# A fused transformer kernel on one core: GpSimd's weight splits in four parts, row normalising moved to ScalarE, the last attention turns reordered

## The chip, the cores and the metric

The kernel runs on one core of one Trainium2 chip. The metric is the device time of one execution in microseconds, as the median of several executions. The core has five engines that run their own instruction streams and wait for one another by semaphores: TensorE (PE in the rows, its weight loads PEld), VectorE (DVE), ScalarE (ACT), GpSimd (POOL) and SyncE (SP), which here issues the DMAs.

## The reference

`x` is 16 sequences of 128 tokens with 256 features. Four residual blocks follow one another:

```python
x = x + tanh(g_xattn[0]) * attention16(layernorm(x), ctx)     # 16 heads, biases, output projection
x = x + tanh(g_ffn[0])   * moe8_dense(layernorm(x))           # 8 experts, all tokens through all experts
x = x + tanh(g_xattn[1]) * attention1(layernorm(x), ctx, mask)# one head of 256
x = x + tanh(g_ffn[1])   * switch(layernorm(x))               # top-1 of 8, capacity 256 rows an expert
```

In the dense mixture each token has eight routing weights. They come from a sigmoid of the router's logits: an exponential of the distance to 1/e inside a zone, a normalised best two where no expert is in the zone, and then a division by their sum. Each expert is `(silu(x Wg) * (x Wu)) Wd` with 256 hidden features. In the last block a token goes to the expert with the largest logit, if it is among the first 256 tokens of that expert, through `relu(x w1) w2` with 1024 hidden features; its result is multiplied by the gate's softmax value.

## The kernel before, in words

Every float32 product is made of three products of "fp32r" halves: a high half (rounded copy) and a low half (difference), so each tensor that TensorE reads is split first. `product` (line 1591) runs the three. Splitting is a copy for the high half and a subtraction for the low one. ScalarE makes the high half of what leaves PSUM (`..._high`, `..._evict`), VectorE the low half (`..._low`); GpSimd makes both halves of the dense experts' weights in `gate_up_split` (1024 columns, lines 2145 and 2147) and `down_split` (512 columns, lines 2153 and 2155), which SyncE then keeps in HBM and reloads for later token groups. The order of work is written out by hand, per engine. Every engine runs its instructions strictly in that order.

The stages:

- **First attention**, steps `b` = 0 to 15, one sequence each, from the start to about 450 us. For each half of the heads TensorE computes scores twice, VectorE takes their maxima (`maximum`, line 1010), GpSimd turns those into a diagonal matrix (`diagonals`, line 2135), which a matmul subtracts, and ScalarE takes the exponential (line 593). `norm1` on VectorE then normalises the row for the experts with a root found by Newton steps (lines 1047 and 1048, three times). `x1_low` (line 1056) hands it to TensorE. From b = 4 the **dense experts** run in between: `gate_up`, `silu`, `h_mult`, `h_high`, `h_low`, `down`, `accumulate` (line 1079), for four groups of four sequences. `zones`, `two_best` and `expert_weights` (lines 1124 to 1145) make a group's routing weights on VectorE, many short instructions in a chain; the first `accumulate` of a group waits for them. `small_ready` (line 937) splits the router weights at b = 4 on VectorE.
- **Experts 25 to 31** of the last group, about 450 to 562 us, with the second attention of groups 0 and 1 begun in between.
- **`turn3`**, three turns `(ga, gb)` = (2, 1), (3, 2), (None, 3), about 562 to 638 us. For `gb`: `probs_transpose`, `attend` (line 1962), `add_attention`, `moments_b`, `root_b` (lines 262 to 267), `normalise_b` (line 1366), `xb_transpose`, `logits1`, `pick_expert` (its last result is `oh_b`), `count_experts`, `places`, `pick_place` (its result is `tok_idx`, line 1418). For `ga`: the projections `k1`, `q1`, `v1`, `scores1`, `mask_and_max`, exponentials. `dispatch` on GpSimd then scatters each token's row (with its scale and shift) to its expert's slot in HBM by indirect DMAs (line 2224).
- **Switch experts**, from about 646 us: SyncE loads the slots back (line 535, first four tiles, then twelve), VectorE normalises two tiles (`slots_norm`, line 1531), TensorE transposes them and runs `hidden` (48 matmuls) and `down4` (48 matmuls, line 2097) per expert, and GpSimd scatters the results (line 2245). ScalarE splits the expert's weights (`split`, line 746), GpSimd (`split_w1`, line 2214) and VectorE (`split_w2`, line 1541) make the low halves, 2048 columns each.

## Time and profile before

| | |
|---|---|
| median of 3 executions | 764.35 us (763.16 to 766.68) |
| the profiled execution | 764.7 us, span 762.9 us from first to last instruction |
| mean granted TensorE clock | 0.921 of full |
| busy: TensorE | 646.4 us (85%) |
| busy: VectorE | 521.0 us (68%) |
| busy: ScalarE | 331.2 us (43%) |
| busy: GpSimd | 229.1 us (30%) |

Busy times are sums of instruction durations without overlap. A share over the whole span mixes stages with different limits, so the stages are read one by one in the timeline. In timeline rows the number in square brackets is the engine's idle time before the instruction, and behind the arrow is what ended it. A clock of 1.00 is 2.4 GHz, 0.50 is 1.2 GHz.

### The profile page before, as it was taken

The page shows a single profiled execution, that of the slowest core. Times are in us where ns is not written, and L with a number is a line of the kernel's source. Part 1 is how long each engine was busy: PE and PEld are TensorE (multiplying, and loading weights), DVE is VectorE, ACT ScalarE, POOL GpSimd, SP SyncE. Part 2 cuts the span into 40 slices and gives each one's busy share as a digit, 9 for nine tenths or more (in the row PEclk, how much of TensorE's full clock was granted, in tenths as well). Part 3 has the DMA queues.
Part 4 walks back from the last instruction along what each step waited for, and adds up shares of the span by engine and source line. Part 5 has one row for each costly group of instructions (what it writes and reads, how often), then busy time and mean ns, then how long its engine had stood idle before and what let it go on. Part 6 is the DMA issues. An engine that isn't in the chain of part 4 may idle for free.

```text
span 762.9 us, 12648 instructions
## 1 busy us (share of the span) xinstructions
PE 646.4 (85%) x4564; PEld 546.7 (72%) x4564; DVE 521.0 (68%) x1362; ACT 331.2 (43%) x530; POOL 229.1 (30%) x155
## 2 busy tenths in 40 slices
PE   5978598899899899999799889999966931799995
PEld 4656366787678778778688777898855821799995
DVE  6877987677877866866776647479458883466662
ACT  4434155355356456456355325152523321455641
POOL 2444624566532212221014010010031242255542
PEclk9879779899999999999999999999989955799998
DMA  7303303335442242333243424434221141964700
GB/s 225 121 15 127 125 1 139 125 135 211 180 166 83 85 165 84 137 113 125 83 165 113 162 87 152 132 124 146 83 69 43 61 161 43 318 210 153 242 20 26
DMA packets 43463, 94.51 MB, mean 124 GB/s; under 512 B 3519, under 2 KB 24383, under 8 KB 42384
## 3 DMA queue, kind: packets, MB, share of 16 engines
q1 hardware_dynamic: 41344, 87.62, 33.6%
q0 software_dynamic: 2064, 6.16, 2.3%
q8 instruction: 33, 0.54, 0.3%
q14 instruction: 22, 0.18, 0.1%
HBM read 72.94 MB, written 21.04 MB: 123 GB/s over the span
## 4 chain that ended last, share of the span: by engine, by line
PE 65%; DVE 24%; issue 5%; ACT 2%; DMA 1%; POOL 1%; DVEq 0%; SPq 0%; ACTq 0%; POOLq 0%
PE psum L1591 43%; PE psum L2097 6%; PE psum L1668 2%; PE psum L1698 2%; PE psum L1628 2%; PE psum L1662 2%; DVE work L1063 1%; DVE scratch L266 1%; DVE x_all L1079 1%; PE psum L1635 1%; PE psum L1647 1%; DVE work L951 1%; PE psum L1962 1%; PE psum L1893 1%; PE psum L1945 1%
## 5 line engine op out<-in xcount | busy, mean ns | idle before, releaser
L1591 PE MATMUL psum<-arena 128*128 128x256 f32 (+1 forms) x2544 | 446.0, 334 | 33.8 <-DVE x_all L1079 15.6
L1591 PEld LDWEIGHTS psum<-arena 128*128 128x128 f32 x2544 | 384.5, 199 | 78.4 <-DVE x_all L1079 14.8
L2135 POOL TENSOR_TENSOR diag<-neg_ident,work 128x1024 fp32r<-128x1024 f32 x32 | 60.9, 1904 | 249.3 <-DVE work L1010 242.5
L1063 DVE TENSOR_TENSOR work<-work,psum 128x512 f32<-128x512 f32 x64 | 43.9, 686 | 62.1 <-PE psum L1591 57.3
L625 ACT ACTIVATE arena<-work 128x512 fp32r<-128x512 f32 x64 | 40.3, 630 | 90.7 <-DVE work L1063 78.7
L1079 DVE SCALAR_TENSOR_TENSOR x_all<-psum,w_exp,x_all 128x256 f32<-128x256 f32 x128 | 55.9, 479 | 27.7 <-PE psum L1591 26.9
L618 ACT ACTIVATE work<-psum 128x512 f32<-128x512 f32 x64 | 38.2, 597 | 56.8 <-PE psum L1591 56.3
L1068 DVE TENSOR_TENSOR arena<-work,arena 128x512 fp32r<-128x512 f32 x64 | 51.8, 810 | 8.7 <-ACT arena L625 8.2
L2218 POOL TENSOR_TENSOR arena<-work,arena 128x1024 fp32r<-128x1024 f32 x4 | 9.5, 2370 | 151.1 <-ACT arena L641 151.1
L1010 DVE TENSOR_REDUCE work<-psum 128x8 f32<-128x1024 f32 x32 | 39.0, 1220 | 15.7 <-PE psum L1647 15.6
L593 ACT ACTIVATE work<-psum 128x1024 f32<-128x1024 f32 x32 | 32.8, 1026 | 35.4 <-PE psum L1668 32.3
L2097 PE MATMUL psum<-arena 128*128 128x256 f32 x384 | 47.9, 284 | 0.0
L2097 PEld LDWEIGHTS psum<-arena 128*128 128x128 f32 x384 | 46.6, 192 | 0.0
L2214 POOL TENSOR_TENSOR arena<-work,arena 128x2048 fp32r<-128x2048 f32 x8 | 37.0, 4621 | 15.9 <-ACT arena L746 15.9
L880 ACT ACTIVATE arena<-psum 128x256 fp32r<-128x256 f32 x64 | 22.6, 385 | 44.1 <-PE psum L1591 43.5
L1545 DVE SCALAR_TENSOR_TENSOR arena<-psum,arena 128x256 fp32r<-128x256 f32 x64 | 24.9, 421 | 20.2 <-ACT arena L880 19.0
L618 ACT ACT_TABLE_LOAD x26 | 33.4, 1283 | 0.5
L746 ACT ACTIVATE arena<-work 128x2048 fp32r<-128x2048 f32 x16 | 30.5, 1907 | 5.1 <-DMA work<-in_w 5.1
L1662 PE MATMUL psum<-arena 32*128 32x256 f32 x384 | 32.6, 303 | 0.2 <-DVE arena L1003 0.2
L2245 POOL DMA_INDIRECT out<-work,out_idx x16 | 15.8, 990 | 51.0 <-DVE work L1556 48.5
L2224 POOL DMA_INDIRECT slots<-x_all,tok_idx x16 | 16.8, 1048 | 42.4 <-DVE tok_idx L1418 38.7
L1662 PEld LDWEIGHTS psum<-arena 32*128 32x128 f32 x384 | 25.9, 192 | 0.8 <-issue 0.8
(194 smaller groups left out, 844.8 us busy)
## 6 DMA issues: line engine op xcount, KB each, us to landing
arena<-kept SPq DMA_DIRECT2D x24, 1024.0 KB, 5.6
work<-in_w SPq DMA_DIRECT2D x16, 1024.0 KB
kept<-arena SPq DMA_DIRECT2D x8, 1536.0 KB, 6.1
arena<-kept SPq DMA_DIRECT2D x24, 512.0 KB, 4.8
work<-in_w SPq DMA_DIRECT2D x8, 768.0 KB, 7.8
slots<-fill POOLq DMA_DIRECT2D x1, 2080.0 KB
work<-in_ctxT SPq DMA_DIRECT2D x8, 256.0 KB, 3.0
work<-in_ctxT SPq DMA_DIRECT2D x4, 512.0 KB, 5.2
```

What stands on the lines that cost most here:

```text
L593: act.activation(probs[u % 2], ps[:, ST:ST + 2, :].rearrange("p j (h q) -> p (j h) q", q=P), ACT.Exp, scale=DH ** -0.5).then_inc(ex, 1)
L618: act.activation(gu[i % 2], ps[:, GA, :], ACT.Silu).then_inc(sl, 1)
L625: act.activation(hT[n % 2][0][:, m, :], gu[i % 2], ACT.Copy).then_inc(hh, 1)
L1010: dve.tensor_reduce(mx[u % 2], ps[:, MX:MX + 2, :].rearrange("p j (h k) -> p (j h) k", k=P), AX.X, ALU.max).then_inc(mx_ok, 1)
L1063: dve.tensor_tensor(gu[i % 2], gu[i % 2], ps[:, UP, :], ALU.mult).then_inc(hm, 1)
L1068: dve.tensor_tensor(hT[n % 2][1][:, m, :], gu[i % 2], hT[n % 2][0][:, m, :], ALU.subtract).then_inc(hl, 1)
L1079: ins = dve.scalar_tensor_tensor(x_all[:, g * GB + t, 0:D], ps[:, DN, j * D:(j + 1) * D], w_exp[g % 2][:, t, e:e + 1], x_all[:, g * GB + t ...
L1591: mm = pe.matmul(dst, left(i, k), right(j, k), start=(n == 0), stop=(n == 3 * K2 - 1))
L1662: pe.matmul(ps[:, ST + j, m * 256:(m + 1) * 256], kT[h % 2][i][r:r + 32, m, t:t + P], qM[h % 2][jj][r:r + 32, m, :, t:t + P], start=False, ...
L2097: mm = pe.matmul(ps[:, 4 + i, j * D:(j + 1) * D], h4[i][a][:, f, j * P:(j + 1) * P], w4[i][b][:, 1, f * D:(f + 1) * D], start=(f == 0 and ...
L2135: pool.tensor_tensor(diag, neg_ident[:, :].rearrange("p (o q) -> p o q", o=1).to_broadcast([P, 8, P]), mx[u % 2].rearrange("p (h o) -> p h ...
L2214: pool.tensor_tensor(w4[i][1][:, 0, :], raw4[i][:, 0, :], w4[i][0][:, 0, :], ALU.subtract).then_inc(w4_l1.sem, 1)
```

## The change

1. **GpSimd's splits in parts.** `gate_up_split` and `down_split` call `split_parts`: four copies and then four subtractions, each over a quarter of the columns. Waits on the counts are multiplied by `PARTS` = 4.
2. **Router weights.** Their zeroing, copy and subtraction go from VectorE's `small_ready` (b = 4) to GpSimd's `router_ready` (b = 1).
3. **Root of `norm1`.** The second instruction of each Newton step becomes a `tensor_scalar` whose last operand is a per-row scalar, in place of a `scalar_tensor_tensor` with a second tensor.
4. **Routing weights.** The first division by the sum and both clampings fall away, and the last division, the gate and the write are one instruction.
5. **Normalising on ScalarE.** `normalise_a`, `normalise_b` and `slots_norm` (but for the first two tiles) become ScalarE activations with a scale and a shift; VectorE makes the shift with one short instruction. The bias of `v1` is added to `x_all` by GpSimd (`value_bias`; rows of the softmax sum to one), so that `v1` is only copied, by ScalarE (`v1_evict`). Row numbers come from constants, so `row_numbers` and three short instructions per turn fall away.
6. **Order of `turn3`.** On TensorE `xa_transpose` and `k1_project` of the next group go to the end of the turn before; `q1_project` comes ahead of `v1_project`, and `scores1` ahead of `xb_transpose`. VectorE does `stats_a`, `moments_a`, `root_a` first in the turn and `mask_and_max` before `xb_low`.
7. **`keep_warm`.** 11 matmuls of 512 bf16 columns, whose results are not used, in the second turn, 35 in the third, and 44 behind it.
8. **First split of the switch experts.** Both low halves for expert 0 are made by VectorE (`first_split`), the second after all rows are dispatched; ScalarE makes both high halves in the last turn.
9. **Slots.** They are loaded in three DMAs (tiles 0 and 1, 2 and 3, the rest).
10. **End.** The last `down4` writes its two halves to different banks and signals the first by itself; `scatter` waits for each half by itself.

The core of the diff:

```diff
+            def split_parts(n, a, z, high, low):
+                i, step = n % 2, (z - a) // PARTS
+                for c in range(a, z, step):
+                    pool.tensor_copy(w2s[i][0][:, c:c + step], raw[i][:, c:c + step]).then_inc(high, 1)
+                for m, c in enumerate(range(a, z, step)):
+                    pool.wait_ge(high, PARTS * n + m + 1)
+                    pool.tensor_tensor(w2s[i][1][:, c:c + step], raw[i][:, c:c + step], w2s[i][0][:, c:c + step], ALU.subtract
+                                       ).then_inc(low, 1)
...
+            def router_ready():
+                pool.wait_ge(s_small, 16 * 7)
+                for i in range(2):
+                    pool.memset(wr[i].bitcast(F32), 0.0).then_inc(s_wr0, 1)
+                pool.wait_ge(s_wr0, 2)
+                pool.tensor_copy(wr[0][:, :, :, 0:E], wr_raw).then_inc(s_wr0, 1)
+                pool.wait_ge(s_wr0, 3)
+                pool.tensor_tensor(wr[1][:, :, :, 0:E], wr_raw, wr[0][:, :, :, 0:E], ALU.subtract).then_inc(s_wr, 1)
...
+            def value_bias(g):
+                pool.wait_ge(s_bo, 2)
+                for t in range(g * GB, (g + 1) * GB):
+                    pool.wait_ge(na, t + 1)
+                    pool.tensor_tensor(x_all[:, t, 0:D], x_all[:, t, 0:D], bv1r, ALU.add).then_inc(xv, 1)
+
             ctx_low(0)
+            value_bias(0)
+            value_bias(1)
+            ctx_low(1)
+            value_bias(2)
             pool.wait_ge(s_disp, 16)
...
+            ctx_low(2)
+            dispatch(0)
+            value_bias(3)
+            ctx_low(3)
+            dispatch(1)
+            dispatch(2)
+            dispatch(3)
...
                 for _ in range(3):
                     step(dve.tensor_scalar(u, r, t, r, ALU.mult, ALU.mult))
-                    step(dve.scalar_tensor_tensor(r, u, 1.5, r, ALU.add, ALU.mult))
+                    step(dve.tensor_scalar(r, u, 1.5, r, ALU.add, ALU.mult))
...
             def expert_weights(g):
-                divide_by_sum(7)
                 seq(dve.tensor_tensor(r[7], r[7], over_e(rs[1]), ALU.mult))
                 seq(dve.tensor_tensor(rt[4], rt[4], rt[7], ALU.add))
-                divide_by_sum(4)
+                seq(dve.tensor_reduce(rs[2], r[4], AX.X, ALU.add))
+                seq(dve.reciprocal(rs[2], rs[2]))
                 if g >= 2:
                     dve.wait_ge(ac, 2 * E * (g - 1))
-                dve.tensor_scalar(w_exp[g % 2], r[4], tgate[:, 2:3], None, ALU.mult).then_inc(s_wexp, 1)
+                dve.scalar_tensor_tensor(w_exp[g % 2], r[4], tgate[:, 2:3], over_e(rs[2]), ALU.mult, ALU.mult
+                                         ).then_inc(s_wexp, 1)
...
+            def normalise_a(g):
+                act.wait_ge(sa, g + 1)
...
+                for t in range(g * GB, (g + 1) * GB):
+                    act.activation(xn_a[t % GB], x_all[:, t, 0:D], ACT.Identity, bias=shiftA[:, t:t + 1], scale=rstdA[:, t:t + 1]
+                                   ).then_inc(na, 1)
...
             def turn3(ga, gb):
+                more = ga is not None and ga + 1 < G
                 probs_copy(gb)
                 if ga is None:
                     act.wait_ge(a1, 2 * G)
                     split(0, 0, 0)
+                    split(0, 0, 1)
                 else:
-                    xa_high(ga)
-                    k1_evict(ga)
                     q1_evict(ga)
+                    if more:
+                        normalise_a(ga + 1)
+                    v1_evict(ga)
+                normalise_b(gb)
                 xb_high(gb)
...
+            def keep_warm(n):
+                for _ in range(n):
+                    pe.matmul(ps[:, 0, :], ident_b[:, :], hide[:, 0:1, :].to_broadcast([P, 4, P]), start=True, stop=True,
+                              skip_group_check=True)
+
             def turn3(ga, gb):
+                more, last = ga is not None and ga + 1 < G, ga is None
                 probs_transpose(gb)
-                if ga is not None:
-                    xa_transpose(ga)
+                if last:
+                    keep_warm(2)
                 attend(gb)
-                if ga is not None:
-                    k1_project(ga)
+                if last:
+                    keep_warm(22)
+                else:
+                    q1_project(ga)
                     v1_project(ga)
-                    q1_project(ga)
+                    scores1(ga)
                 xb_transpose(gb)
-                if ga is not None:
-                    scores1(ga)
+                if more:
+                    xa_transpose(ga + 1)
+                else:
+                    keep_warm(5)
                 logits1(gb)
+                if not more:
+                    keep_warm(2)
                 logits1_transpose(gb)
+                if more:
+                    k1_project(ga + 1)
+                else:
+                    keep_warm(4)
                 places(gb)
+            xa_transpose(2)
+            k1_project(2)
             turn3(2, 1)
             turn3(3, 2)
             turn3(None, 3)
+            keep_warm(44)
...
+                        if more and f == 3:
+                            act.wait_ge(s_xs[1 + i], 16)
+                            slots_norm(*nxt)
```

## Rows read from the trace of the kernel before

**Rows 1.** Stages: us; busy of PE, PEld, DVE, ACT, POOL; clock; DMA.

```profile
72.00:100.00 28.00, 18.85 (x138) 12.76 (x136) 24.97 (x64) 6.77 (x12) 15.87 (x14) 0.75 0.33 114
100.00:136.00 36.00, 29.13 (x195) 22.86 (x193) 28.79 (x79) 18.42 (x30) 12.15 (x9) 0.93 0.20 74
136.00:450.00 314.00, 292.98 (x2176) 242.34 (x2176) 223.92 (x561) 157.45 (x226) 92.39 (x65) 0.98 0.38 134
450.00:563.00 113.00, 103.60 (x598) 90.39 (x597) 71.30 (x200) 43.71 (x72) 11.09 (x7) 0.97 0.34 114
608.00:648.00 40.00, 12.23 (x49) 8.23 (x48) 23.37 (x74) 8.71 (x17) 13.38 (x9) 0.55 0.29 96
```

**Rows 2.** Timeline, 82 to 92 us: start us, us, engine, line, operation, idle before.

```profile
82.14 0.28 DVE L1047 TENSOR_SCALAR work<-work 128x1 f32<-128x1 f32 x1
82.17 2.36 POOL L2147 TENSOR_TENSOR arena<-work,arena 128x1024 fp32r<-128x1024 f32 x1
82.45 2.10 DVE L1048 SCALAR_TENSOR_TENSOR work<-work 128x1 f32<-128x1 f32 x1
...
85.15 1.03 ACT L593 ACTIVATE work<-psum 128x1024 f32<-128x1024 f32 x1 [2.20 <-PE psum L1668]
...
91.41 1.65 PE L1591 MATMUL psum<-arena 128*128 128x256 f32 x6 [2.20 <-DVE arena L1025]
```

**Rows 3.** GpSimd's groups: count, busy us, mean ns, idle before.

```profile
L2147 POOL TENSOR_TENSOR arena<-work,arena 128x1024 fp32r<-128x1024 f32 x8 | 19.4, 2423 | 0.6
...
L2160 POOL TENSOR_TENSOR x_all<-x_all,biasr 128x256 f32<-128x256 f32 x16 | 12.2, 764 | 0.0
```

**Rows 4.** Timeline, the first group's routing, 117 to 140 us.

```profile
122.50 2.22 DVE L1097 TENSOR_TENSOR work<-work 128x32 f32<-128x32 f32 x1
...
136.24 9.34 PE L1591 MATMUL psum<-arena 128*128 128x256 f32 x48 [2.88 <-DVE x_all L1079]
```

**Rows 5.** Timeline, the second group's routing, 254 to 262 us.

```profile
254.80 0.18 DVE L1103 TENSOR_REDUCE work<-work 128x4 f32<-128x32 f32 x1
...
258.26 4.00 PE L1591 MATMUL psum<-arena 128*128 128x256 f32 x31 [2.59 <-DVE x_all L1079]
```

**Rows 6.** Timeline, four scaled copies on ScalarE and two bf16 matmuls.

```profile
29.46 1.70 ACT L586 ACTIVATE arena<-arena,parity 128x256 fp32r<-128x256 f32 x4
...
35.39 0.61 PE L1628 MATMUL psum<-hide,ident_b 128*128 128x512 bf16 x2
```

**Rows 7.** Timeline of the second and third turns, 591 to 639 us.

```profile
591.50 0.21 PE L1986 MATMUL psum<-oh_b,tri_b 128*128 128x32 bf16 x1 [6.27 <-DVE oh_b L1398]
...
594.25 2.18 PE L1962 MATMUL psum<-work 128*128 128x256 f32 x8
...
613.44 3.78 PE L1962 MATMUL psum<-work 128*128 128x256 f32 x8 [0.69 <-ACT work L780]
...
618.51 1.91 ACT L746 ACTIVATE arena<-work 128x2048 fp32r<-128x2048 f32 x1 [5.13 <-DMA work<-in_w]
...
620.51 4.49 POOL L2214 TENSOR_TENSOR arena<-work,arena 128x2048 fp32r<-128x2048 f32 x1 [1.51 <-ACT arena L746]
620.63 4.38 DVE L266 SCALAR_TENSOR_TENSOR scratch<-scratch,work 128x4 f32<-128x4 f32 x1
...
630.33 2.90 PE L1591 MATMUL psum<-arena 128*128 128x512 f32 x6 [1.46 <-ACT arena L787]
...
638.06 0.16 DVE L1418 TENSOR_TENSOR tok_idx<-work,tokn 128x4 int32<-128x4 f32 x1
```

**Rows 8.** GpSimd's dispatches (ns min/median/max), slots' first load, first expert.

```profile
L2224 POOL DMA_INDIRECT slots<-x_all,tok_idx x16: 964/969/2112, 555.8 to 643.5; - x16
...
646.11 3.75 DMA x_all<-slots
...
653.60 8.67 PE L1591 MATMUL psum<-arena 128*128 128x256 f32 x48 [1.80 <-DVE arena L1536]
```

**Rows 9.** Timeline, the last scatter.

```profile
757.17 0.98 POOL L2245 DMA_INDIRECT out<-work,out_idx  x1 [0.30 <-issue]
```

More of the change, by code:

```diff
@@ L335, in block_kernel @@
         oh1, loc1, dest = sem("onehot_ready"), sem("places_ready"), sem("rows_ready")
-        s_xs = [sem("first_slots_loaded"), sem("other_slots_loaded")]
+        s_xs = [sem(f"{n}_slots_loaded") for n in ("first", "second", "other")]
         s_raw4 = [sem(f"expert1_weights_loaded{i}") for i in range(2)]
@@ L827, in _ @@
             silu(29, 1)
+            v1_evict(1)
             h_high(29, 1)
+            normalise_b(0)
+            xb_high(0)
             silu(30, 0)
-            xb_high(0)
             h_high(30, 0)
@@ L862, in turn3 @@
                 gate_exp(gb)
+                if more:
+                    xa_high(ga + 1)
+                if more:
+                    k1_evict(ga + 1)
+            xa_high(2)
+            k1_evict(2)
             turn3(2, 1)
@@ L880, in hidden, with slots_norm @@
                 act.activation(h4[i][0][:, f, :], ps[:, f % 4, 0:CAP], ACT.Relu).then_inc(h1_hi.sem, 1)
+            def slots_norm(g, i):
+                for j in range(2):
+                    row = xs[:, bass.ds(4 * g + 2 * i + j, 1), :].rearrange("p a c -> p (a c)") if not isinstance(g, int) \
+                        else xs[:, 4 * g + 2 * i + j, :]
+                    act.wait_ge(xd_t.sem, xd_t.now(g, 1) if i else xd_t.before(g, 2))
+                    act.activation(xd[j], row[:, 0:D], ACT.Identity, bias=row[:, D + 1:D + 2], scale=row[:, D:D + 1]
+                                   ).then_inc(xd_ok.sem, 1)
             def turn(g, last):
@@ L1380, in xb_low @@
                                       ).then_inc(nb_lo, 1)
-            top, rank, gate, row, place, own = (r3s[i] for i in range(6))
+            top, rank, gate, row, place = (r3s[i] for i in range(5))
             def over8(col):
@@ L1513, in turn3 @@
                     root_a(ga + 1, 1)
-                    normalise_a(ga + 1)
+                attention_gates(gb)
+                add_attention(gb)
+                moments_b(gb)
+                root_b(gb)
+                if ga is not None:
+                    mask_and_max(ga)
+                xb_low(gb)
+                if ga is None:
+                    first_split(0, w4_l1.sem)
                 pick_expert(gb)
-                count_experts(gb)
+                slot_and_gate(gb)
                 pick_place(gb)
+                if more:
+                    xa_low(ga + 1)
+            xa_low(2)
             turn3(2, 1)
@@ L2091, in down4 @@
                 pe.wait_ge(y4.sem, y4.before(g, i + 1))
+                if last:
+                    pe.wait_ge(y4.sem, y4.now(g, 1))
                 for j in range(2):
+                    bank = 4 if last and j else 4 + i
                     for f in range(8):
@@ L2106, in turn @@
                         slots_transposed(*((g, 1) if i == 0 else (g + 1, 0)))
-                    down4(g, i)
+                    down4(g, i, last and i == 1)
             slots_transposed(0, 0)
```

221 lines of the change are left out of this document (94 added, 127 removed).

## Prediction

> **What bounds it.** I read the busy time and the granted clock by stage first [rows 1], and then the timeline wherever TensorE stands idle. From 136 to 450 us TensorE is busy 293 of 314 us: only its rare waits can be won there. Before that, and from 563 to 653 us, VectorE sets the end. From 608 to 648 TensorE works 12 of 40 us at 0.55 of its clock, which is the lower level (1.2 GHz) for nearly all of it. So each edit is asked one thing: does it shorten a wait of TensorE in one of these stretches? The last stage, from 653 us, is TensorE's again.
>
> **72 to 100 us.** In [rows 2] the second `L1048` (VectorE, one element, two tensor inputs from SBUF) takes 2.10 us, and it ends with GpSimd's `L2147`. `L1047` beside it, the same size with scalars in place of the second tensor, takes 0.28. So the scalar form of the root update saves some 2 us of VectorE here. It has a price: against the 0.16 us of an undisturbed `L1048` I take +0.07, between 0 and the 0.12 by which `L1047` is longer. That is 0.2 us per norm, and some five of the sixteen norms are on the path: +1.0 (0 to +1.8). The router weights leave VectorE too: `small_ready` stands before `o_low(3)`, and TensorE starts at 91.41 having waited 2.20 us for it [rows 2]. Of both savings not all arrives. ScalarE's exponential (85.15, 1.03 us [rows 2]) stands before `x1_high` and so holds `x1_low`; through `o_normalise` and `o_back`, `out_project` then starts near 89.1 instead of 91.4: **-2.3** (-3.5 to 0). On GpSimd `router_ready` is about 1.6 us (four small instructions, by [rows 3]) at b = 1, where GpSimd waits for VectorE's maxima: nothing.
>
> **The four parts.** A subtraction of 1024 columns takes 2.42 us, one of 256 takes 0.76 [rows 3], so some 0.2 us is fixed per instruction. Twelve more instructions per expert are up to 2.5 us, 20 us of GpSimd for eight experts, less what overlaps. GpSimd works 12 of 36 us and 92 of 314 [rows 1], so this is covered unless VectorE is held by it. What VectorE wins is less than it looks. Before, one small two-input operation lost 2 us and the next ones were free (`L1097` at 122.50, 2.22 us [rows 4]); now each meets a part of its own and loses some 0.5. Only a large one, 0.7 us by itself and held for 2, wins clearly. TensorE waited 2.88 us behind this chain [rows 4]; I take -0.7 there (0 to -3.9), and -1.0 (0 to -3) for the rest up to 250 us. The Trainium skill (SBUF — State Buffer, Who interferes with whom) says that the side which issues first keeps the shared port pair for its whole instruction while the other blocks fully, and that a VectorE instruction with at most one SBUF input, outside the 2-port modes, does not contend. The rows of `L1048` and `L1047` agree; by that rule alone a chain of small operations gains nothing, and this term would be 0 instead of -0.7.
>
> **Expert weights.** `expert_weights` falls from eleven VectorE instructions to five, each about 0.22 us with the gap behind it (`L1103` takes 0.18 [rows 5]): -1.35 us. TensorE waits 2.59 us for the accumulation behind it [rows 5], and nothing else stands close behind. Four groups: **-5.4**. With fewer waits before 140 us the clock, at 0.75 over 72 to 100 [rows 1], may stay up longer; -1.0 (0 to -4).
>
> **450 to 563 us.** ScalarE takes `normalise_a` (four at 1.70 us by [rows 6]) and `v1_evict`; GpSimd takes `value_bias`, 16 x 0.76 = 12.2 us [rows 3]. TensorE sets this stage (it waits for few things), so the moves gain nothing. They cost something at its end: behind `silu(31,1)`, `normalise_a(2)` delays `h_high(31,1)` and so `down(31,0)` by 0.7 us, and `value_bias(2)` and `ctx_low(2)` may hold VectorE: +1.0 (0 to +2).
> To 563 us: -2.3 +1.0 -0.7 -1.0 -5.4 -1.0 +1.0 = **-8.4**.
>
> **The three turns of turn3.** Marks of before: `attend(2)` ends at 596.4, `attend(3)` at 617.2, the last `tok_idx` is begun at 638.06 [rows 7].
> - First turn, -2.8. `xa_transpose(2)` and `k1_project(2)` go where TensorE waited for the exponentials. VectorE does `stats_a(3)` and its root ahead of group 1's chain, and `value_bias(3)` can hold that chain: `logits1(1)` is 1.1 us later. But TensorE's wait of 6.27 us for `oh_b` [rows 7] was caused by the same work standing before `pick_expert`; `k1_project(3)` (3.0 us) now fills half of it. That is -6.3 +3.0 +1.1 = -2.2; the transposes of `xa` (1.9) are gone from before `attend(2)`, but `probs_copy(2)` waits for `k1_evict(3)` (+1.3).
> - Second turn, -2.6. `k1_project` (-3.0) and `xa_transpose` (-1.9) are gone from it; 5 warming matmuls (two take 0.61, overlapped, so 0.22 each [rows 6]) and the later ones add 1.1; `v1_evict` before `normalise_b` on ScalarE waits for `v1_project`: +1.2.
> - Third turn, -6.7, from 21.0 us. GpSimd's first subtraction of 2048 columns (4.49 us) held `L266` for 4.38 [rows 7]: -4.2. It is now on VectorE behind `xb_low` and fits into logits, copy and transposes (3.1 us). `logits1(3)` took 2.90 at the lower clock [rows 7], 1.5 at the full one: -1.4. The other transposes and matmuls at full clock give -0.7, three VectorE instructions fewer -0.6, ScalarE's slower normalising +0.2. Its two splits (1.91 each) need weights that landed some 10 us after their issue (ScalarE waited 5.13 us for them, to 618.51 [rows 7]); issued near 601 they are there before the normalising.
> Together **-12.1** (-15 to -4).
>
> **Dispatch and first slots.** One dispatch took 2.11 us where the median is 0.97 [rows 8], while VectorE ran `L1541`; that subtraction now waits until the dispatch is over: **-1.1**. Two tiles of slots instead of four land some 0.9 us sooner (3.75 us for four), the transposes at full clock take 0.5 less, and the first 48 matmuls 5.8 instead of 8.67 [rows 8]. Against this, ScalarE's split behind the second `hidden` comes some 1.6 us before expert 1's weights, whose load starts no sooner after the dispatch: it is late next, and costs 2.0. Sum **-2.3** (-4.5 to 0). From there each half turn is TensorE's; `slots_norm` on ScalarE (0.9 us behind the fourth `hidden`) is done before the transposes need it: 0.
>
> **Tail.** The last two row scatters were issued 0.98 + 0.30 = 1.28 us apart [rows 9], after both tiles; now the first goes during the second half of `down4`, and one of two sums (0.45) is off the end too: **-1.7**.
>
> **Sum.** -8.4 -12.1 -1.1 -2.3 -1.7 = -25.6 on the profiled execution's 764.7 us (span 762.9 and 1.8 around it): 739.1. The median shown is 0.35 lower; I say **739**.
>
> **Rivals.**
> (a) Chance 0.17, about 731: the stalls and the lower clock before 140 us go almost wholly (another -6), and the weights are in time (-2). For it: TensorE's waits there are larger than what I take.
> (b) Chance 0.15, about 748: the order written for ScalarE becomes the wait. `v1_evict` stands before `normalise_b` and waits for TensorE; if each turn loses 3 us to such queues, 9 of the 12 us are lost. Against it: ScalarE worked only 9 of the 40 us from 608 [rows 1].
> (c) Chance 0.08, about 751: the clock stays low in spite of the warming matmuls. Then 22 of them take 10 us and 44 take 20, past the arrival of the slots by 8, and the clock's gains (4) are lost: +12.
> (d) Chance 0.05, the other side, about 771: the 20 us (parts) and 12.2 us (bias) that GpSimd adds fall on VectorE, each two-input operation waiting for one of its instructions. Whole, it gives 739 + 32. It decides only if over four fifths of that time is on the path; against it, most of it runs where TensorE is the bound.
>
> Mine has 0.55, in 733 to 745. Case (a) reaches to 727, (b) and (c) to 752; outside remain (d) and the edges. What a measurement of this kernel can tell from no change is about 0.5%, 3.8 us: only (d) gives the same or slower, split 0.02 and 0.03.
>
> **What would show it.** No `L1048` over 0.3 us; GpSimd's parts at 0.4 to 0.8 us with short VectorE stalls; 1.3 us of wait before a group's first accumulation; the last `tok_idx` near 618 (638.1 - 8.4 - 12.1); the full clock from the last `attend` to the first slots; one scatter after the last matmul. It would be wrong if the last turn waits in ScalarE's queue, if warming matmuls still run when the slots are there, or if TensorE has new waits for VectorE between 136 and 450.

## The result, and the profile after

The changed kernel takes 737.8 us (737.4 to 743.0, four executions) against 763.8 (761.9 to 766.7): ratio 0.967, interval 0.962 to 0.971. The forecast was 739, in a range of 727 to 752. A second set of six gave 740.6 (732.9 to 742.3) against 760.6, ratio 0.970 (0.965 to 0.974).

The profiled execution of the changed kernel is its slowest (743.0, span 741.2), so its span fell by 21.7 us where the medians fell by 26.0 (and by 20.0 in the second set). Why executions of one program differ is part of the findings. The stages of the changed kernel, columns as in [rows 1]:

```profile
72.00:100.00 28.00, 19.76 (x151) 13.56 (x150) 24.93 (x66) 8.73 (x13) 19.30 (x26) 0.85 0.42 147
100.00:136.00 36.00, 30.18 (x202) 24.16 (x201) 29.41 (x76) 17.96 (x29) 15.86 (x28) 0.93 0.21 74
136.00:450.00 314.00, 296.41 (x2186) 245.09 (x2185) 216.40 (x547) 160.87 (x232) 105.82 (x134) 0.97 0.38 135
450.00:563.00 113.00, 105.23 (x617) 91.03 (x616) 66.48 (x189) 54.60 (x99) 16.72 (x17) 1.00 0.36 119
...
604.00:632.00 28.00, 21.99 (x101) 10.29 (x99) 14.02 (x42) 7.32 (x11) 5.75 (x6) 0.92 0.30 94
632.00:643.00 11.00, 9.51 (x56) 9.30 (x57) 2.91 (x8) 5.53 (x12) 3.08 (x1) 0.73 1.06 368
```

GpSimd works 105.8 us between 136 and 450 (92.4 before, [rows 1]), and TensorE is none the worse for it: it is busy for 296.4 us against 293.0. The last two rows are the new weak places: the clock is 0.92 in the last turn and 0.73 in the first slots' matmuls.

The groups of the root and of GpSimd's parts (columns as in [rows 3]), in which the root's second instruction is now `L1101` and the subtraction `L2190`:

```profile
L1100 DVE TENSOR_SCALAR work<-work 128x1 f32<-128x1 f32 x48 | 13.1, 273 | 1.7
...
L1101 DVE TENSOR_SCALAR work<-work 128x1 f32<-128x1 f32 x48 | 10.3, 214 | 1.7
...
L2190 POOL TENSOR_TENSOR arena<-work,arena 128x256 fp32r<-128x256 f32 x32 | 25.3, 819 | 0.0
...
L2190 POOL TENSOR_TENSOR arena<-work,arena 128x128 fp32r<-128x128 f32 x32 | 13.7, 459 | 0.0
```

No instruction of `norm1`'s root is held any more, where [rows 2] had one of 2.10 us. The price is 0.214 - 0.16 = 0.05 us each; I had taken 0.07. A quarter of the subtraction takes 0.82 us, not 2.42 / 4 = 0.61.

TensorE's waits before each group's first accumulation, in the timeline:

```profile
133.95 8.22 PE L1609 MATMUL psum<-arena 128*128 128x256 f32 x41 [1.94 <-DVE x_all L1132]
...
252.60 7.34 PE L1609 MATMUL psum<-arena 128*128 128x256 f32 x48 [1.59 <-DVE x_all L1132]
...
368.95 1.68 PE L1609 MATMUL psum<-arena 128*128 128x256 f32 x12 [1.48 <-DVE x_all L1132]
...
472.59 9.66 PE L1609 MATMUL psum<-arena 128*128 128x256 f32 x64 [1.20 <-DVE x_all L1132]
```

The first two answer to [rows 4, 5], which have 2.88 and 2.59; in all four groups before the waits were 2.88, 2.59, 2.83 and 2.83, and they are now 4.9 us shorter in sum. The turns, in the timeline, with `L1980` the matmuls of `attend` and `L2067` the warming ones:

```profile
591.22 2.06 ACT L776 ACTIVATE work<-x_all 128x256 f32<-128x256 f32 x4
...
592.32 1.47 PE L1911 MATMUL psum<-cst,work 128*128 128x128 f32 x8
...
601.00 1.99 PE L1980 MATMUL psum<-work 128*128 128x256 f32 x8 [0.26 <-ACT work L812]
...
602.84 4.91 PE L2067 MATMUL psum<-hide,ident_b 128*128 128x512 bf16 x22
...
609.09 2.11 PE L1911 MATMUL psum<-cst,work 128*128 128x128 f32 x8 [1.35 <-ACT work L776]
...
612.78 2.35 PE L1609 MATMUL psum<-arena 128*128 128x512 f32 x6
...
619.34 0.16 DVE L1440 TENSOR_TENSOR tok_idx<-work,cst 128x4 int32<-128x4 f32 x1
```

The last `tok_idx` is at 619.3 where [rows 7] have 638.1. The first transposes of `xb` in the second turn (592.32) follow scores without a gap, although ScalarE's normalising ahead of them was behind `v1_evict`. And the first slots: timeline first, with the warming matmuls (617.77), the transposes, the first `hidden` matmuls and ScalarE's split (`L762`), then one piece of the chain that ended last:

```profile
617.77 9.66 PE L2067 MATMUL psum<-hide,ident_b 128*128 128x512 bf16 x44
...
629.44 0.66 PE L2112 MATMUL psum<-cst,work 128*128 128x128 f32 x4 [2.01 <-DVE work L1549]
...
631.90 7.22 PE L1609 MATMUL psum<-arena 128*128 128x256 f32 x36 [1.81 <-DVE arena L1554]
...
637.92 1.91 ACT L762 ACTIVATE arena<-work 128x2048 fp32r<-128x2048 f32 x1 [2.67 <-DMA work<-in_w]
...
640.61 1.71 PE L1609 MATMUL psum<-arena 128*128 128x256 f32 x12 [1.49 <-DVE arena L1563]
```

```profile
627.48 10.33 DMA work<-in_w
```

What released the split is a weight load that takes 10.3 us of the chain. [rows 8] had the slots' load there instead. The end, in the timeline, against [rows 9]:

```profile
732.61 0.98 POOL L2313 DMA_INDIRECT out<-work,out_idx  x1 [6.35 <-DVE work L1579]
...
735.42 0.98 POOL L2313 DMA_INDIRECT out<-work,out_idx  x1 [1.82 <-DVE work L1579]
```

One scatter is left behind the last matmul (734.0).

### The profile page after: what moved, and what is told of

Same layout as the page of the kernel before. It is cut to its first block, busy times and chain, and to the rows that moved or that the text cites. A ratio compares the mean times of both kernels' runs of the same rounds, so it can differ in the third digit from the quotient of the medians.

```text
span 741.2 us, 12936 instructions
## 1 busy us (share of the span) xinstructions
PE 659.5 (89%) x4654; PEld 548.0 (74%) x4654; DVE 485.6 (66%) x1269; ACT 356.4 (48%) x584; POOL 252.2 (34%) x270
## 4 chain that ended last, share of the span: by engine, by line
PE 62%; DVE 23%; issue 6%; ACT 4%; DMA 2%; POOL 1%; ACTq 0%; SPq 0%; DVEq 0%; POOLq 0%
PE psum L1609 41%; PE psum L2139 6%; PE psum L1716 2%; PE psum L1686 2%; PE psum L1646 2%; PE psum L1680 2%; DVE x_all L1132 2%; DVE work L1116 2%; PE psum L1653 1%; DMA work<-in_w 1%; DVE work L1004 1%; PE psum L1665 1%; DVE work L1100 1%; PE psum L1723 1%; DVE scratch L266 1%
## 5 line engine op out<-in xcount | busy, mean ns | idle before, releaser
L1116 DVE TENSOR_TENSOR work<-work,psum 128x512 f32<-128x512 f32 x64 | 43.8, 685 | 66.1 <-PE psum L1609 60.3
L1121 DVE TENSOR_TENSOR arena<-work,arena 128x512 fp32r<-128x512 f32 x64 | 48.8, 763 | 10.1 <-ACT arena L630 9.7
L2290 POOL TENSOR_TENSOR x_all<-x_all,biasr 128x256 f32<-128x256 f32 x16 | 11.2, 732 | 85.5 <-ACT work L648 85.5
L2190 POOL TENSOR_TENSOR arena<-work,arena 128x256 fp32r<-128x256 f32 (+1 forms) x64 | 38.9, 639 | 0.0
L2273 POOL TENSOR_TENSOR arena<-work,arena 128x2048 fp32r<-128x2048 f32 x7 | 32.5, 4646 | 15.4 <-ACT arena L762 15.4
L762 ACT ACTIVATE arena<-work 128x2048 fp32r<-128x2048 f32 x16 | 30.4, 1905 | 4.8 <-DMA work<-in_w 2.7
```

Of the source, the lines that this page charges most:

```text
L1116: dve.tensor_tensor(gu[i % 2], gu[i % 2], ps[:, UP, :], ALU.mult).then_inc(hm, 1)
L1121: dve.tensor_tensor(hT[n % 2][1][:, m, :], gu[i % 2], hT[n % 2][0][:, m, :], ALU.subtract).then_inc(hl, 1)
L2190: pool.tensor_tensor(w2s[i][1][:, c:c + step], raw[i][:, c:c + step], w2s[i][0][:, c:c + step], ALU.subtract).then_inc(low, 1)
```

## The experiments

Each was timed over five to eleven executions. The whole times of one kernel scatter by 4 to 12 us, so I read the stages of the profiled execution as well. The table has, in us: start to first transposes of `norm1(0)`; from there to those of `norm1(3)` (A); to the end of the accumulations (B); to the end of `attend(3)` (C); to the last `tok_idx` (D); to the start of the last dispatch (E); to the first `hidden` (F); its 48 matmuls (G); to the end of the span (H).

```
                    start   A     B     C     D    E    F     G    H     span   median  ratio (95%)
before              50.8  46.5 465.5  54.4  21.0  5.3 10.1   8.7 100.6  762.9
changed             53.7  43.2 457.8  48.3  16.5  4.1  8.3  10.4  98.9  741.2   737.8  .967 (.962-.971)
e1 the same         51.6  43.3 457.9  48.2  16.5  4.1  8.5  10.3  98.9  739.3   740.6  .970 (.965-.974)
e2 one part         54.0  44.8 461.6  47.6  15.5  4.0  8.7  10.2  98.9  745.3   742.2  .975 (.972-.978)
e3 no warming       51.8  39.6 459.2  50.8  16.9  4.1  8.9   8.7  98.9  738.9   740.7  .973 (.970-.976)
e4 old root         51.5  45.2 457.0  48.4  16.5  4.0  8.5  12.0  99.4  742.5   740.4  .972 (.968-.975)
e5 old weights      50.8  41.7 466.5  48.5  16.5  4.0  8.7  10.6 100.1  747.4   748.7  .983 (.979-.987)
e6 before + head    51.2  43.3 459.2  54.3  21.0  5.3 10.3   7.8 100.6  753.0   754.3  .987 (.984-.991)
e7 early w1         54.4  42.4 457.9  48.3  16.5  4.1  8.5   8.6  98.8  739.5   737.4  .966 (.962-.970)
e8 and warming      51.5  43.0 458.0  47.6  15.4  4.1  8.7   7.0  98.8  734.1   735.3  .964 (.961-.968)
e9 and early warm   53.4  43.0 457.9  48.2  16.5  4.1  8.7   6.8  98.9  737.5   734.1  .959 (.956-.963)
e10 last turn only  51.4  40.6 457.9  49.7  15.2  4.0 10.5   8.8  98.9  737.0   742.3  .970 (.967-.974)
e11 eight parts     51.5  39.0 457.3  48.4  16.5  4.1  8.7  10.2  98.8  734.5   738.3  .966 (.962-.969)
e12 GpSimd split    54.9  39.7 456.9  48.3  20.8  4.1  8.7   8.8  98.9  741.1   743.2  .971 (.967-.976)
```

Ratios are to the kernel before on the same chip (760.6, 762.9 and 766.0 us in the three sets: e1 to e4, e5 to e8, e9 to e12). The changed kernel itself was timed again in the first set alone, so medians of e5 to e12 are compared with it across chips. Each row's stages come from one profile.

**e1, the changed kernel again.** 

> The changed kernel once more, as the base of the ratios of this study. Its four executions so far were 743.0, 737.8, 737.8 and 737.4, with a clock of 0.953 in the first and 0.96 in the others. If the low stretches of the clock fall anew in each execution, this profile shows them in other places and the time is 736 to 743 again. If they are bound to the program, the profile shows 27 to 37, 51 to 61 and 133 to 140 us again, and 743.

In the first 100 us the low stretches moved. Windows of the changed kernel's first profile and of e1's, the same code (granted clock is the third number from the end):

```profile
27.00:37.00 10.00, 9.19 (x48) 6.88 (x50) 7.09 (x16) 4.42 (x8) 4.35 (x3) 0.50 0.01 2
```

```profile
27.00:37.00 10.00, 8.35 (x99) 6.07 (x97) 9.92 (x18) 5.60 (x10) 4.57 (x3) 1.00 0.01 2
```

At the lower level TensorE does 48 matmuls in this window, at the upper one 99. Up to 563 us, e1, e3, e7, e8, e10 and e12 also run the code of the changed kernel. Over these seven profiles start and A together take 91.4 to 96.9 us, and B 456.9 to 459.2. So the first 100 us scatter by 5.5 us, and the next 460 by 2.3. That may be the larger part of the spread of the whole times (9.3 us in e1), but the other executions have no profile to show it.

Behind 100 us the low stretches of e1 are those of the first profile, each 2 us earlier like the work itself: 130 to 138, 315 to 319 and 441 to 449 us against 132 to 140, 317 to 321 and 443 to 451. There the clock falls at the same instructions in this pair. It isn't bound to them for good: e3 and e12, the same code again, have a low stretch between 215 and 222 us and none near 315.

A finer measure than B is the step from one sequence's transposes of `norm1` to the next one's. For `norm1(3)` to `norm1(7)`, in which GpSimd still splits weights for the experts (us):

```
                      3 to 4   4 to 5   5 to 6   6 to 7
before                  35.6     33.1     28.4     29.8
changed, e1, e7, e10    34.6     32.6     27.3     27.9
e3, e12                 34.4     32.4     27.3     28.5
e8                      35.7     32.1     27.3     27.9
e2 one part             35.9     33.5     28.4     28.7
e4 old root             34.4     32.5     27.3     28.1
e11 eight parts         35.4     29.6     29.9     28.9
```

**e2, one part.** 

> PARTS is 1: GpSimd's halves in one instruction each, all else as in the changed kernel. Mine: VectorE's two-input operations are held up to 2.2 us again, against twelve fewer instructions of GpSimd per expert: 1.7 us slower than the changed kernel (0 to 7), 739.5. Rival 'the stalls go wholly with the parts' (a): 4 to 7 slower, 742 to 745. Rival 'a chain of small operations gains nothing from parts': 0, 737.8. Rival 'the fixed cost of the parts lands on VectorE' (d in small): faster, below 736.

```diff
-PARTS = 4
+PARTS = 1
```

B is 3.7 us longer than in e1 and 2.4 longer than in any profile of the same code. (A is 1.5 longer, within its scatter.) The four steps of the table above take 126.5 us in sum against 122.4 to 123.0 in the same code with four parts, and behind them every step is within 0.1 us of one seen there. So parts gain 3.5 to 4.1 us while GpSimd splits. The held instruction is back, in the timeline:

```profile
124.55 2.42 POOL L2190 TENSOR_TENSOR arena<-work,arena 128x1024 fp32r<-128x1024 f32 x1
...
125.00 2.02 DVE L1153 TENSOR_TENSOR work<-work 128x32 f32<-128x32 f32 x1
```

With four parts the same line takes 0.78 at 122.2, but its neighbours lose 0.1 to 0.5 us each there. From the start of `L1116` to that of `L1189` this chain takes 13.4 us with one part (from 121.17) and 13.2 with four (from 118.24), and TensorE's waits before the first accumulations are the same in both: 1.94, 1.59, 1.48 and 1.20. So the chain of small operations gains 0.2 us, which is near the nothing of the second rival. What gains is elsewhere: from `norm1(3)` to the second group's routing VectorE's `h_low` (`L1121`, 512 columns) takes 18.9 us with one part and 16.2 with four, and `L1056` 5.9 against 4.1. `h_low` over the whole run, in the changed kernel, in e2 and in e11:

```profile
L1121 DVE TENSOR_TENSOR arena<-work,arena 128x512 fp32r<-128x512 f32 x64 | 48.8, 763 | 10.1 <-ACT arena L630 9.7
...
L1121 DVE TENSOR_TENSOR arena<-work,arena 128x512 fp32r<-128x512 f32 x64 | 51.9, 811 | 11.1 <-ACT arena L630 10.7
...
L1121 DVE TENSOR_TENSOR arena<-work,arena 128x512 fp32r<-128x512 f32 x64 | 54.8, 857 | 10.3 <-ACT arena L630 10.0
```

The medians differ by 1.5 us (742.2 against 740.6), near the 1.7 forecast, but the ratios' intervals overlap. By the stages the parts are worth twice what I took, and a little less than rival (a) of 4 to 7.

**e3, no warming.** 

> All warming matmuls are left out, all else as in the changed kernel. Mine: the clock is at its lower level from the last attend to the middle of the first slots' matmuls; logits 1.4, other transposes and matmuls of the turn 0.7, slots' transposes 0.5, and the first 48 matmuls up to 1 (they were partly slow with the warming too): 3 to 4 us slower, 741 to 742. Rival (c), the warming does not keep the clock: 0 or up to 1 faster, since 11 matmuls of the second turn fall away (736.5 to 738). Rival, the warming gives all of the gain of the third turn: 6 or more slower.

```diff
 def keep_warm(n):
-    for _ in range(n):
+    for _ in range(0):
```

```profile
590.00:640.00 50.00, 23.07 (x104) 17.70 (x105) 21.75 (x72) 16.25 (x32) 10.06 (x9) 0.59 0.49 170
```

The forecast was 3 to 4 us slower. C is 2.6 longer (against e1), D 0.4, F 0.4; G is 1.6 shorter. The clock is low over nearly the whole stretch, and 1.8 us of C to G are lost in all. G starts 0.4 us later here after the last dispatch, and the clock came back at 635 us, 3.7 us into it; in e1 it fell at 629 and came back at 636, 5.9 us into it. So part of what the warming had won was given back in G. The whole times differ by 0.1; A, 3.7 shorter by its place in the clock, hides the rest in the profile. So no gain of the warming shows in the whole time. Rival (c), a clock that stays low in spite of the warming, is refuted for the turns: 590 to 601 and 604 to 635 us are low here, and only 608 to 613 and 629 to 636 in e1.

**e4, old root.** 

> The root of norm1 has its two-tensor scalar_tensor_tensor back, all else as in the changed kernel, so GpSimd's work is in parts. Mine: against one part it would cost 2; against quarter parts it loses some 0.5 us per norm that meets a part and gains 0.2 where none is met: within 1 us of the changed kernel, 737 to 739. Rival 'the scalar form only costs' (the parts alone cure the stall): 1 us faster, 736.8. Rival 'the scalar form is worth its 2 us still': 2 us slower, 739.8.

```diff
-step(dve.tensor_scalar(r, u, 1.5, r, ALU.add, ALU.mult))
+step(dve.scalar_tensor_tensor(r, u, 1.5, r, ALU.add, ALU.mult))
```

A is 1.9 longer, B 0.9 shorter than in e1. A's share is within its scatter. B's is likely the price of the longer instruction, forecast at 1.0: the five profiles with the new root and their low stretches at the same instructions (changed, e1, e7, e9, e10) have 457.8 or 457.9. The whole times (740.4 and 740.6) don't tell the two roots apart. With the parts in place, no gain of the scalar form is shown; in these two profiles it is 1.0 us. What it is worth against unsplit GpSimd work was not tried by itself.

**e5, old routing weights.** 

> Routing weights by the eleven instructions of before (two divisions, two clampings), all else as in the changed kernel. Mine: TensorE's wait before a group's first accumulation grows by 1.35 us in each of four groups, 5.4 by the end of the accumulations, and 5.4 on the span. Rival 'the chain has other cover': the waits grow by less, 2 us or under in all. Rival 'stalls multiply the chain': more than 2 us a group, 8 or more. The mark to read is the gap between the marks before and after each group's first accumulation, since the clock of the first 100 us moves everything by up to 5 us.

```diff
+divide_by_sum(7)
 seq(dve.tensor_tensor(r[7], r[7], over_e(rs[1]), ALU.mult))
 seq(dve.tensor_tensor(rt[4], rt[4], rt[7], ALU.add))
-seq(dve.tensor_reduce(rs[2], r[4], AX.X, ALU.add))
-seq(dve.reciprocal(rs[2], rs[2]))
+divide_by_sum(4)
...
-dve.scalar_tensor_tensor(w_exp[g % 2], r[4], tgate[:, 2:3], over_e(rs[2]), ALU.mult, ALU.mult
+dve.tensor_scalar(w_exp[g % 2], r[4], tgate[:, 2:3], None, ALU.mult
```

B is 8.6 us longer and the median 8.1 (11.3 against e7 on the same chip, whose weights come earlier too): more than the 5.4 forecast. Two of the four waits, and the clock where these groups begin, in e5 and then in e1:

```profile
249.42 8.80 PE L1611 MATMUL psum<-arena 128*128 128x256 f32 x48 [2.76 <-DVE x_all L1132]
...
368.48 1.74 PE L1611 MATMUL psum<-arena 128*128 128x256 f32 x12 [2.76 <-DVE x_all L1132]
```

```profile
249.00:257.00 8.00, 7.58 (x44) 7.28 (x45) 4.78 (x9) 1.57 (x4) 3.94 (x3) 0.79 0.24 68
367.00:379.00 12.00, 9.32 (x44) 8.28 (x45) 6.21 (x13) 1.23 (x2) 1.90 (x1) 0.72 0.13 44
```

```profile
250.00:258.00 8.00, 7.37 (x50) 6.70 (x51) 5.91 (x12) 2.07 (x4) 3.94 (x3) 1.00 0.22 68
366.00:378.00 12.00, 9.79 (x92) 8.14 (x94) 7.36 (x14) 3.02 (x5) 1.90 (x1) 1.00 0.33 108
```

The four waits are 2.88, 2.76, 2.76 and 2.48 against 1.94, 1.59, 1.47 and 1.19 in e1: 4.7 us. Most of the rest is clock: it fell behind the second and third of these waits, and these two windows stayed at the upper level in e1. The step from one `norm1` to the next in which the second wait stands is 2.5 us longer than in e1, and the third's 3.7, where the waits themselves grew by 1.2 and 1.3: 3.8 us. 4.7 + 3.8 = 8.5. That the longer waits brought the clock down is my reading, and the kernel before speaks against its being a rule: it had waits of 2.59 at 258 us and of 2.83 at 374 and kept its clock, and its two steps are longer than the changed kernel's by 0.9 and 1.4, the waits alone.

**e6, before with the head's edits alone** (parts, router weights, root, routing weights). 

> The kernel before with four edits alone: parts, router weights by GpSimd, scalar form of the root, shorter routing weights. Nothing of normalising, turn3, warming, slots or end. Mine: the end of the accumulations 9.4 us earlier than before (8.4 and the 1.0 that ScalarE's normalising was to cost there), and the span 9.4 shorter, near 752. Rival 'edits multiply' (the first half only pays with the reordering behind it): under 6 us of the span. Rival 'normalise_a on ScalarE cost nothing': the accumulations end where the changed kernel ends them, 8.1 earlier.

The median is 8.6 lower, the span 9.9, the end of the accumulations 9.1; forecast 9.4. The rest of the change takes another 11.8 us off the span. B falls by 6.3 with the head's edits and by another 1.4 in the changed kernel, which is what one low stretch more in e6 (546 to 550 us, at half speed 2 us) costs. From the last group's first accumulation to the last one e6 takes 84.2 us and e1 82.2, and that stretch of low clock is the difference. So the moves to ScalarE and GpSimd between 450 and 563 us cost nothing that shows, where I had +1.0.

**e7 and e8, weights early, more warming.** 

> The changed kernel, but the first matrix of the second switch expert is loaded right after the last attend, into columns that are free by then, and ScalarE's first split waits for that load alone; its second matrix comes in two halves at the old place. Mine: ScalarE's wait of 2.67 us for weights goes, TensorE's 1.49 behind it too, so the first 48 matmuls take 1.5 to 2.5 us less: 1.5 to 2.5 faster than the changed kernel by the mark at their end. Rival 'the slots are late next': the early load and the last dispatches share the queues, and the gain is 0. Rival 'nothing, the wait is hidden': the first down4 starts at the same distance behind the slots.

> As e7, and 53 warming matmuls in place of 44 behind the last turn, and 8 more behind the slots' transposes, so that TensorE does not stand from 627.4 to 631.9. Mine: the clock stays at its upper level through the first 48 matmuls (7.6 us of them ran behind such a stand in part at the lower one), which then take near 6 us: 2 to 3 us less than e7. Rival 'the warming delays the transposes': they start later by what the ninth matmul overhangs, and the gain is under 1. Rival 'the clock falls anyway': no change against e7.

```diff
+sp.wait_ge(a1, 2 * G)
+sp.wait_ge(x3, B)
+sp.dma_start(raw4[1][:, 0, :]..., w1[slice(1, 2)]...).then_inc(s_w1, 16)
 sp.wait_ge(s_disp, 16 * B + 16)
...
-    load4(1, slice(1, 2))
+    for c in range(2):
+        sp.dma_start(raw4[1][:, 1, 1024 * c:1024 * (c + 1)]..., w2[slice(1, 2)]...).then_inc(s_raw4[1], 16)
...
-keep_warm(44)
+keep_warm(53)
...
 slots_transposed(0, 0)
+keep_warm(8)
```

The last two pairs are e8's alone. ScalarE's split stands in a loop whose counter is a register, so the condition that should make it wait for the early load alone never held: in what ran it waits for the second matrix, whose halves now travel without the first. Nothing waits for the early load, which was issued at 604.4 us in e7 and took 6.6 us; a version for use needs SyncE to wait on it before it goes on. G fell from 10.4 to 8.6 in e7 (no wait of ScalarE before the split) and to 7.0 in e8, where the clock stayed up. First `hidden` and chain of e8:

```profile
628.29 4.57 PE L1620 MATMUL psum<-arena 128*128 128x256 f32 x36
```

```profile
623.54 7.26 DMA work<-in_w
```

The 36 matmuls take 4.57 us and not 7.22. The load is still on the chain, with 7.3 us in place of 10.3: 0.5 us of ScalarE's wait are left in e8. From the last `tok_idx` on, e8 takes 118.6 us and the changed kernel 121.7. The median of e8 is 735.3; its interval overlaps that of the changed kernel. e8 has both edits to the warming, so it doesn't tell the 53 from the 8.

**e9, warming in the first 100 us too.** 

> As e8, with 8 and 6 warming matmuls more in the first 100 us, where TensorE waits 4.12 us (at 48 us) and 3.15 us (at 78 us) for normalised rows of x. Mine: the low stretches at 47 to 54 and 78 to 81 us, which follow these waits, shorten or go; 3 to 5 us of clock at half speed are worth 1 to 2.5 us, and the executions scatter less than the 4.8 us of e8. Rival 'the clock of this stretch is set by something else': the low stretches stay and the 14 matmuls run at the lower clock, 0.43 us each, and delay the transposes: 0 to 1 us slower. Rival 'VectorE sets this stretch': the clock is up and the marks do not move.

```diff
+if b % 2:
+    keep_warm(9 - b, UP)
 second_piece(b, UP)
```

A is 43.0 as in e8, and start is 1.9 longer, with a low stretch at 27 to 37 us that lies ahead of the first added matmul. The stretch of e8 at 77 to 81 is gone, and A is the same to 0.1 us, as the rival 'VectorE sets this stretch' has it; but A scatters by 3.7 in the same code, so a gain of 1 to 2.5 us could not be seen in one profile. The executions scatter by 7.1 us, more than the 4.8 of e8 and not less. Its ratio, 0.959, is the lowest of all, but nothing in the stages puts that down to this edit. e8 and e9 are the fastest versions run, both without the wait named under e7. e9's interval (0.956 to 0.963) lies below e1's and overlaps that of the first four executions (from 0.962) by a hair.

**e10, warming in the last turn only.** 

> The changed kernel without the 11 warming matmuls of the second turn; those of the third turn and behind it stay. After e3, where attend(2) to attend(3) took 21.2 us and 17.9 with the warming: if these 11 hold the clock there, 3 us slower between these two marks, and the rest as in the changed kernel. By my prediction (they cost 1.1 us and gain nothing): 1.1 faster. Rival 'it was the chance place of a low stretch in e3': no change beyond 1 us.

```diff
-    keep_warm(5)
+    keep_warm(5 if last else 0)
```

(and so for the 2 and 4 behind it.) C is 1.5 us longer, D 1.3 shorter, for the dip of the clock came at 596 to 599 instead of 611 to 614. So the eleven matmuls neither cost the 1.1 that I had nor hold the clock for good; in this pair they moved a low stretch from the second turn to the third. (F is 2 us longer; 1.5 of it is the last dispatch, which landed 4.0 us after its start and not 2.5, and which the edit doesn't touch.)

**e11, eight parts.** 

> PARTS is 8. Twenty-four... instructions more of GpSimd per expert than with 4, each with some 0.2 us of its own: 4.8 us per expert, of which GpSimd has room. VectorE's holds shrink from 0.5 to 0.3 us at most. Mine: within 1.5 us of the changed kernel to the last accumulation. Rival 'the shorter the better' (the stall is all): 1.5 to 3 faster. Rival 'GpSimd's time is the next bound': 2 or more slower, with TensorE waiting for the low halves of gate and up in steps 5 to 8.

(Against four parts it is sixteen instructions more per expert, not twenty-four.) B is 457.3 against 457.9. Its groups:

```profile
L2190 POOL TENSOR_TENSOR arena<-work,arena 128x128 fp32r<-128x128 f32 x64 | 28.4, 478 | 0.0
...
L2190 POOL TENSOR_TENSOR arena<-work,arena 128x64 fp32r<-128x64 f32 x64 | 19.1, 333 | 0.0
```

GpSimd's subtractions take 47.5 us instead of 39.0, and for the first time TensorE waits for them. From the waits of e11 (us, times, longest):

```profile
PE psum L1609 <- POOL arena L2190: 4.3, 3, 2.4
```

Four parts have no such line. `h_low` is longer too, 857 ns on average against 763 (rows under e2). The four steps of the table under e1 take 123.8 us against 122.4 to 123.0. That B is the same in spite of this goes with the clock: over B it is short of full speed by 6.8 us in e11 and by 10.2 to 11.9 in the same code with four parts. Why it is higher here is open. So no gain of eight parts shows, and while GpSimd splits they lose about 1 us.

**e12, GpSimd's first split again.** 

> The changed kernel, but the first low half of the switch experts is made by GpSimd again, ahead of its last dispatches, as before the change. Mine: its 4.5 us meet VectorE's root of the last turn, one two-input instruction of L266 to L268 takes over 3.5 us instead of 0.16, and the last tok_idx and the end come 3.5 to 4.2 us later. Rival 'it falls beside the root here': no instruction of VectorE over 1 us there, and 0 or a little later through the wait of the last dispatches. Rival 'VectorE wins back its own 2.28 us': under 2 later.

```diff
-if ga is None:
-    first_split(0, w4_l1.sem)
...
 dispatch(2)
+split_w1(0, 0)
 dispatch(3)
```

```profile
602.63 5.22 DVE L263 TENSOR_SCALAR work<-work 128x4 f32<-128x4 f32 x1
...
603.32 4.50 POOL L2271 TENSOR_TENSOR arena<-work,arena 128x2048 fp32r<-128x2048 f32 x1
```

D is 20.8, 4.3 longer. This one instruction takes 5.22 us where it takes 0.17 in the changed kernel, and VectorE no longer makes the low half behind it. The size is near the forecast; the victim is not as forecast. I had named two-input instructions, and `L263` has one tensor and two constants.

## Why the prediction was right, step by step

Its time and range held: 739 against 737.8 and 740.6. But the sum it rests on was -25.6 us on the profiled execution, and the spans fell by 21.7 (first profile) and 23.6 (e1); the medians fell by 26.0 and 20.0. The terms, against before and the first profile after:

- **72 to 100 us, -2.3, with the longer norm +1.0 and the clock -1.0.** A fell by 3.3. `out_project` begins at 89.5 in e1 against 91.4 and waited 1.00 us against 2.20, though the transposes nine us ahead of it began 0.7 later (80.08 against 79.36): 2.6 us won, near the 2.3. How much of it is the root, the router weights or the parts was not taken apart. (The held instruction of [rows 2] is the third `L1048` of that norm, not the second.) The price of the longer norm, +1.0, is near the 0.9 by which B differs in e4. The start's +2.9 is the scatter of the first 100 us: the same code has 51.4 to 54.9.
- **The four parts, -0.7 and -1.0: mis-sized.** e2 shows 3.5 to 4.1 in place of 1.7, and not where I put it: the -0.7 for the wait before the first accumulation measured 0 (1.94 us with one part as with four), and the -1.0 for the rest up to 250 us measured all of it. The mechanism that I named is right: the small operations of a chain win next to nothing, and the large one does. Its size was too low; `h_low` alone takes 2.7 us less. Against before, the four steps of the table under e1 fell by 4.4, 0.9 of it the first group's wait, and so show the same size.
- **Expert weights, -5.4.** The waits fell by 4.9 against before and differ by 4.7 in e5, and the instructions' own time is well read. The 8.6 of e5 holds 3.8 of clock that the kernel before did not lose, so it is not what this edit brought here. For the same reason the single figures of e2 and e5 (12.3) don't add up to the 7.7 by which B fell.
- **450 to 563 us, +1.0: not borne out.** No cost of the moves shows (e6).
- To 563 us: -8.4 forecast, -8.1 in the profile, -10.0 in e1. The parts, sized too small, and the cost of the moves, sized too large, both pull to the side of a larger gain: A and B gave 11.0. The late start of this execution, 2.9, brought it back to 8.1.
- **The turns, -12.1: measured -10.6** (from the last accumulation to `tok_idx`: 75.4 to 64.8). The first two turns gave 6.1 (C) for 5.4. The third gave 4.5 (21.0 to 16.5) where the step says 6.7. Its largest term, 4.2 for the split taken from GpSimd, measured 4.3 (e12). What failed is the full clock: a dip at 611 to 614 made `logits1(3)` take 2.35 and the transposes 2.11; in e8 without the dip D is 15.4, which leaves 1.1 of the 6.7 unexplained. The second turn's 11 warming matmuls cost 0 and not 1.1 (C and D of e10 together against e1).
- **Dispatch, -1.1: measured -1.2.**
- **First slots, -2.3: measured -0.1.** F gave 1.8. The load of expert 1 was late, as forecast, and e7 sizes it at 1.8 (2.0 forecast). The step that failed is "the first 48 matmuls 5.8 instead of 8.67": TensorE stood still from 627.4 to 631.9 but for four transposes, the clock fell with the first `hidden`, and they took 10.4. e7 and e8 show the halves: with the weights sooner 8.6, and without such a stand too 7.0.
- **Tail, -1.7: measured -1.7** (8.9 to 7.2 us behind the last matmul).

Rival (a): no, since the clock of the first 100 us stayed as it was (0.83 before, 0.84 after, over 10 to 100 us). Rival (b): no; ScalarE normalised behind `v1_evict`, and TensorE was busy until 592.3 anyway. Rival (c): no; the clock held through most of the turns (e3) and fell for long only behind the 4.5 us in which no warming matmul ran, but a dip at 610 to 614 came in spite of the warming. Rival (d): no; TensorE waits nowhere for a split of GpSimd, and with one part in place of four the kernel is slower, not faster (e2).

The agreement of the total is thus partly luck: the parts and the cost of the moves were off to one side, the third turn and the first slots to the other, by 1 to 2 us each, and the medians of the two sets lie on either side of the forecast.

## What to carry to other kernels

Before a chain of short instructions is cut up, look for the long instruction on the neighbouring engine that holds it: cutting that one in four gave about 4 us here, and cutting it in eight nothing more. But the gain was with the large instructions, not with the chain: measure both. Warming matmuls should last until the real work begins; here 4.5 us of standing between the two brought the clock down again (`hidden` at 8.6 us in e7, 7.0 in e8). And compare stages, not whole times, when the start of one program scatters more than the edit is worth.

## What the hardware showed beyond that

One-tensor instructions of VectorE can be held by GpSimd too. In the changed kernel the root over two sequences begins with `L263`, of two columns:

```profile
L263 DVE TENSOR_SCALAR work<-work 128x2 f32<-128x2 f32 x8 | 7.5, 944 | 0.1
...
L263 DVE TENSOR_SCALAR work<-work 128x4 f32<-128x4 f32 x6 | 2.3, 380 | 0.1
```

The first takes 0.94 us on average (0.17 alone, and each held one ends with an instruction of GpSimd), while none of the 48 `L1100` of one column passed 0.28 us, and in e12 the form of four columns was held 5.22 us. The Trainium skill (SBUF — State Buffer, Who interferes with whom) says so: a VectorE instruction with at most one SBUF input escapes only outside the 2-port modes, and `copy`, `cast` and `tensor_scalar` can enter such a mode. These rows agree: two and four columns were held, one was not. My prediction quoted the exception and did not use it. Whether two instructions of one column each would do better than `L263` of two was not tried; 8 x 0.8 = 6 us of VectorE hang on it.

The place of the low clock in the first 100 us is not the program's: the same code had 0.50 or 1.00 over 27 to 37 us. The Trainium skill (TensorE: Matmul & The Clock Gate, Part 1) says of the slow matmuls at a kernel's start that their number varies between runs of one kernel, and puts that ramp under one per cent of a typical span. The trace agrees that it varies, and shows more than a start ramp: low stretches come and go up to 100 us. The starts of the same code differ by 5.5 us, 0.7% of 740.
